# Expert weights of a mixture layer: split in the background by GpSimd, and blocks run by expert rank

## The reference

```python
# layer 1: attention of each token over itself and 77 context tokens (one head)
s_self = jnp.einsum('bsh,bsh->bs', q, k_tok)[..., None]
s_ext = jnp.einsum('bsh,beh->bse', q, k_ext)
probs = jax.nn.softmax(jnp.concatenate([s_self, s_ext], axis=-1), axis=-1)
ctx = probs[..., :1] * v_tok + jnp.einsum('bse,beh->bsh', probs[..., 1:], v_ext)
# layer 2: self-attention (16 heads of 32), and beside it 8 experts, 2 per token
attn = jax.nn.softmax(jnp.einsum('bqhd,bkhd->bhqk', q, k) / jnp.sqrt(hd), axis=-1)
attn_out = jnp.einsum('bhqk,bkhd->bqhd', attn, v).reshape(B, S, D)
gate = jax.nn.softmax(x @ W_gate + b_gate, axis=-1)
top_g, top_i = jax.lax.top_k(gate, TOP_K)
combine = jnp.sum(jax.nn.one_hot(top_i, E) * top_g[..., None], axis=2)
moe_out = jnp.einsum('bsef,bse->bsf', jnp.einsum('bsd,edf->bsef', x, W_experts) + b_experts, combine)
return attn_out + moe_out          # each expert's matrix is 512 x 512
```

## Time and profile before

| | us |
|---|---|
| median of 3 runs | 1459.54 |
| lowest, highest | 1453.82, 1528.65 |
| profiled execution, its own time | 1458.29 |
| its span, first to last instruction | 1456.7 |
| TensorE busy | 1324.4 (91%) |
| VectorE busy | 945.7 (65%) |
| ScalarE busy | 903.1 (62%) |
| GpSimd busy | 365.8 (25%) |

### The profile page before, as it was taken

One profiled execution on the slowest core, in us unless ns is written; L12 is line 12 of the kernel. 1 busy time (PEld: TensorE's weight loads), 2 busy tenths in 40 slices (PEclk: granted clock), 3 DMA queues, 4 the chain that ended last, 5 costly groups with the idle time before them and its releaser, 6 DMA issues.

```text
span 1456.7 us, 25076 instructions
## 1 busy us (share of the span) xinstructions
PE 1324.4 (91%) x6720; PEld 971.6 (67%) x6721; DVE 945.7 (65%) x2019; ACT 903.1 (62%) x1828; POOL 365.8 (25%) x580
## 2 busy tenths in 40 slices
PE   4989999999789899999999999999997769999997
PEld 4968888888565566565665656656563347777776
DVE  4256878787388877777777777777776734333432
ACT  4123434344258889899888998989997743333332
POOL 0001222221100040111101110011113027677775
PEclk9899999999899999999999999999997679999999
DMA  5004444447645344473454733447336277787774
GB/s 158 1 18 160 171 166 158 165 159 265 247 120 141 80 104 132 89 179 80 89 133 90 187 80 87 125 100 188 76 91 181 16 239 131 130 144 135 134 135 65
DMA packets 101293, 187.43 MB, mean 129 GB/s; under 512 B 27257, under 2 KB 35577, under 8 KB 99939
## 3 DMA queue, kind: packets, MB, share of 16 engines
q1 hardware_dynamic: 69984, 138.86, 33.1%
q0 software_dynamic: 26624, 42.04, 17.2%
q10 hardware_dynamic: 4611, 5.74, 1.4%
HBM read 71.09 MB, written 69.35 MB: 96 GB/s over the span
## 4 chain that ended last, share of the span: by engine, by line
PE 70%; issue 7%; ACT 7%; DMA 7%; DVE 6%; POOL 1%; ACTq 1%; POOLq 0%; SPq 0%; DVEq 0%
PE banks L216 14%; PE banks L218 13%; PE banks L217 13%; PE banks L1042 9%; PE banks L1026 6%; PE banks L1006 6%; ACT plain L732 3%; ACT banks L722 3%; DMA out_dram<-plain,score_bias 2%; DMA plain<-h_rows,score_bias 2%; PE banks L1099 2%; DVE plain L1465 1%; PE banks L894 1%; PE banks L927 1%; DMA plain<-in_L_xattn_Wq_dram 1%
## 5 line engine op out<-in xcount | busy, mean ns | idle before, releaser
L216 PE MATMUL banks<-parts 128*128 128x512 f32 (+6 forms) x1108 | 437.5, 395 | 30.0 <-issue 7.5
L218 PE MATMUL banks<-parts 128*128 128x512 f32 (+6 forms) x1108 | 423.8, 383 | 0.0
L217 PE MATMUL banks<-parts 128*128 128x512 f32 (+6 forms) x1108 | 423.8, 382 | 0.0
L1465 DVE TENSOR_REDUCE plain<-banks 128x1 f32<-128x512 f32 x512 | 329.1, 684 | 74.6 <-PE banks L1006 71.6
L722 ACT ACTIVATE banks<-banks,plain 128x512 f32<-128x512 f32 x512 | 338.7, 662 | 43.0 <-DVE plain L1465 40.6
L732 ACT ACTIVATE plain<-banks 128x1024 f32<-128x1024 f32 x256 | 262.5, 1026 | 40.9 <-PE banks L1026 39.2
L216 PEld LDWEIGHTS banks<-parts 128*128 128x128 f32 (+1 forms) x1108 | 214.4, 193 | 74.8 <-issue 36.5
L218 PEld LDWEIGHTS banks<-parts 128*128 128x128 f32 (+1 forms) x1108 | 214.0, 193 | 40.4
L217 PEld LDWEIGHTS banks<-parts 128*128 128x128 f32 (+1 forms) x1108 | 215.1, 194 | 34.4
L1006 PE MATMUL banks<-parts 96*128 96x512 f32 x512 | 208.9, 446 | 27.3 <-ACT banks L722 26.6
L1026 PE MATMUL banks<-parts 104*128 104x512 f32 x512 | 176.2, 426 | 15.1 <-ACT plain L732 14.0
(11 more groups left out here) (167 smaller groups left out, 1417.6 us busy)
## 6 DMA issues: line engine op xcount, KB each, us to landing
parts<-parts SPq DMA_DIRECT2D x384, 128.0 KB, 2.4
h_turned<-parts SPq DMA_DIRECT2D x32, 512.0 KB, 3.0
parts<-h_turned SPq DMA_DIRECT2D x32, 512.0 KB, 7.2
plain<-in_x_dram SPq DMA_DIRECT2D x32, 256.0 KB, 3.0
out_dram<-plain SPq DMA_DIRECT2D x32, 256.0 KB, 2.0
h_rows<-plain SPq DMA_DIRECT2D x32, 256.0 KB, 2.0
parts<-plain SPq DMA_DIRECT2D x8, 1024.0 KB, 4.6
out_dram<-plain POOLq DMA_DIRECT2D x16, 512.0 KB, 6.2
```

Source lines behind the costliest of these rows:

```text
L216: pe.matmul(out, stat[0], mov[0], start=first, stop=False)
L217: pe.matmul(out, stat[0], mov[1], start=False, stop=False)
L218: return pe.matmul(out, stat[1], mov[0], start=False, stop=last)
L1465: dve.tensor_reduce(nmx[:, k, t:t + 1], bank[SB[t]][:], AX.X, ALU.max, negate=True).then_inc(q["f_max"], 1)
```

## The change

- A new array in memory, `experts_split` (`ws_dram`), holds each expert's two parts. GpSimd fills it during the attention, expert by expert, in chunks of 128 rows: it loads a chunk (256 KB), rounds it, subtracts, and writes 512 KB (`load_chunk`, `split_chunk`). Experts 0 and 1 are split in batch 0, one in each of batches 1 to 5 (two chunks in each half), and the last in batch 6. The scatters of the list (`place`) run earlier: all 16 groups by batch 5.
- VectorE's routing ranks the experts by their number of blocks. Each rank has a fixed place in `parts`; blocks are run rank by rank.
- SP reads the list and loads the experts by rank in the last batch, each by one transfer of 2 MB whose address comes from a register. Rank 0 goes before the batch's stacks, the others as their places come free.
- The splitting of experts by ACT and DVE is gone, and so are ACT's four issues at step 6. ACT issues the biases' load after its last copy of the attention.
- PE's wait in the expert stage is for a count that is a constant per group of 8 blocks (`m_ready`). The loops of PE, ACT and DVE there hold 8 blocks in place of 4.
- GpSimd fetches the first four blocks' rows early in the last batch, before its last two `attended`.
- In `score` the key products come before the self-score products, with a semaphore of their own (`s_keys`).

```diff
-        EB = (0, EW, 3 * EW, r4 - EW, 2 * EW, r0, r4, r4 + EW)
+        EB = (0, r4 - EW, EW, 3 * EW, 2 * EW, r0, r4, r4 + EW)
+        chunk = [area(parts, r4 + EW + 4 * S + 2 * D * i, 2, D) for i in range(2)]
@@ sync @@
+            def load_expert(r):
+                if r == 0:
+                    sp.wait_ge(q["r_ranked"], 1)
+                    for i in range(2):
+                        sp.wait_ge(q[f"ws_out{i}"], 16 * NE * C // 2)
+                e = sp.value_load(ranked[0:1, r:r + 1], min_val=0, max_val=NE - 1)
+                sp.dma_start(ew[r], ws_dram[bass.ds(e, 1)].rearrange("e p n -> p (e n)")).then_inc(q[f"in_ew{r}"], 16)
...
                 sp.dma_start(V, Vst).then_inc(q["f_v_in"], 16)
+                if last:
+                    read_list()
+                    load_expert(0)
                 stacks(b, 1, 0, (0, 3), number(b, "R1")[0] + 1)
...
+                if last:
+                    load_expert(1)
+                    sp.wait_ge(q["f_d_full"], number(b, "R3")[0] + 1)
+                    load_expert(2)
+                    load_expert(3)
+                    for slot in (0, 1, 2, 4):
+                        sp.wait_ge(q[f"f_stack{slot}"], (2 * B if slot < 3 else B) * FILL)
+                    load_expert(4)
+                    sp.wait_ge(q["f_t_full"], T * (NH * b + 12))
+                    load_expert(5)
+                    sp.wait_ge(q["f_t_full"], T * (NH * b + 14))
+                    load_expert(6)
+                    sp.wait_ge(q["f_t_full"], T * (NH * b + NH))
+                    load_expert(7)
@@ gpsimd @@
+            def split_chunk(e, c):
+                n = e * C + c
+                pool.wait_ge(q[f"ws_in{c % 2}"], e * (C // 2 * 16) + c // 2 * 16 + 16)
+                pool.tensor_copy(chunk[c % 2][:, 0], full(chunk[c % 2][:, 1])).then_inc(q["ws_hi"], 1)
+                pool.wait_ge(q["ws_hi"], n + 1)
+                pool.tensor_tensor(chunk[c % 2][:, 1], full(chunk[c % 2][:, 1]), full(chunk[c % 2][:, 0]), ALU.subtract).then_inc(q["ws_lo"], 1)
+                pool.wait_ge(q["ws_lo"], n + 1)
+                pool.dma_start(ws_dram[bass.ds(e, 1)].rearrange("e p (a c n) -> p (e a) c n", a=2, c=C)[:, :, c, :],
+                               full(chunk[c % 2])).then_inc(q[f"ws_out{c % 2}"], 16)
...
+            with pool.Fori(1, B - 2) as b:
+                place(PER * b - PER + 1)
+                split_expert(b + 1, True, range(C // 2))
                 attended(b, 0)
+                for m in range(1, PER):
+                    place(PER * b - PER + 1 + m)
+                split_expert(b + 1, True, range(C // 2, C))
                 attended(b, 1)
...
             for i in range(4):
                 fetch(i)
+            attended(B - 1, 0)
             attended(B - 1, 1)
@@ scalar @@
-                    if last and k == 6:
-                        act.wait_ge(q["ew_moved"], 16)
-                        act.wait_ge(q["f_d_full"], number(b, "R3")[0] + 1)
-                        for e in range(EARLY):
-                            act.dma_start(full(ew[e][:, 1]), we_dram[e].rearrange("(c p) n -> p c n", p=P)).then_inc(q[f"in_ew{e}"], 16)
...
+            act.dma_start(be_all, b_exp.rearrange("(a e) n -> a (e n)", a=1).broadcast_to([P, NE * D])).then_inc(q["in_be"], 16)
@@ vector @@
-                            if last and k >= NH - 2 * EARLY:
-                                expert_lo((k - NH + 2 * EARLY) // 2, range(k % 2 * C // 2, (k % 2 + 1) * C // 2))
...
-            LATER = {0: over_tiles_1, 1: over_tiles_2, 2: over_tiles_3, 3: first_blocks_1, 4: first_blocks_2, 6: places, 7: first_records,
-                     8: second_records, 11: block_experts, 12: block_firsts, 13: block_order, 14: list_zero}
+            LATER = {0: over_tiles_1, 1: over_tiles_2, 2: over_tiles_3, 3: first_blocks_1, 4: first_blocks_2, 5: rank_places, 6: places, 7: first_records,
+                     8: second_records, 10: block_experts, 11: block_places, 12: block_firsts, 13: block_order, 14: list_zero}
@@ tensor @@
-                    if part == "first":
-                        e = pe.value_load(bexp[0:1, bass.ds(i, 1)], min_val=0, max_val=NE - 1)
-                        pe.wait_ge(q["m_elo"], e * C + C if k < 2 else NE * C)
+                    if k == 0:
+                        pe.wait_ge(q["m_ready"], n + 1)
```

More of the change, by code:

```diff
@@ L320, in program @@
         N_PICKED = 19
-        EARLY = NE // 2
+        U = 8
+        BULK = NB // U
+        assert NB % U == 0 and T * B * 2 >= U * NE
         @block.sync
@@ L420, in _ @@
             batch(B - 1, False, True)
[L422 to L435, removed]
+            for r in range(NE):
+                sp.wait_ge(q[f"in_ew{r}"], 16)
+                sp.sem_inc(q["m_ready"], BULK if r == NE - 1 else 1)
             for i in range(NB):
@@ L790, in blocks @@
             def blocks(n, part):
-                for k in range(4):
-                    i = 4 * n + k
-                    if not (part == "first" and k == 0) and not (part == "last" and k == 3):
+                for k in range(U):
+                    i = U * n + k
+                    if not (part == "first" and k == 0) and not (part == "last" and k == U - 1):
                         rows_hi(i + 1, (k + 1) % 2)
@@ L799, in _ @@
                 rows_hi(i, i)
-            for e in range(EARLY, NE):
-                expert_hi(e, range(C))
             blocks(0, "first")
-            with act.Fori(1, NB // 4 - 1) as n:
+            with act.Fori(1, BULK - 1) as n:
                 blocks(n, "middle")
-            blocks(NB // 4 - 1, "last")
-            weighted(NB - 1, 3, NB // 4 - 1)
+            blocks(BULK - 1, "last")
+            weighted(NB - 1, 3, BULK - 1)
         @block.tensor
@@ L897, in score @@
                                      start=False, stop=c == C - 1)
+                last.then_inc(q["s_keys"], 1)
+                for c in range(C):
+                    last = prod3(pe, bank[1][:, c * P:D], at(hT[u % 2], sl, c), at(A, sl, c, slice(c * P, D)), c == 0, c == C - 1)
                 last.then_inc(q["s_full"], 1)
@@ L1102, in blocks @@
             def blocks(n, part):
[L1103 to L1105 removed]
+                for k in range(U):
+                    i = U * n + k
+                    if part != "last" or k < U - 1:
                         await_ge(pe, "m_hT", i)
[L1108 removed]
+                        rows_turn(i + 1, U // 4 * n + (k + 1) // 4, k + 1)
                     pe.wait_ge(q["m_hT"], i + 1)
@@ L1122, in _ @@
             blocks(0, "first")
-            with pe.Fori(1, NB // 4 - 1) as n:
+            with pe.Fori(1, BULK - 1) as n:
                 blocks(n, "middle")
-            blocks(NB // 4 - 1, "last")
+            blocks(BULK - 1, "last")
         @block.vector
@@ L1370, in _ @@
             small = [row[:, 7 * NT + NE * i:7 * NT + NE * (i + 1)] for i in range(4)]
-            run, blk, start, base = (t_in, t_lg)[(NT - 1).bit_length() % 2], small[0], small[1 + NE.bit_length() % 2], small[3]
-            ends = small[2 - NE.bit_length() % 2]
+            run = (t_in, t_lg)[(NT - 1).bit_length() % 2]
+            blk, start, ends, base = small
+            ranks = t_sel.rearrange("p t e -> p (t e)")
+            pairs, key, rank, place_of = ranks[:, 0:NE * NE].rearrange("p (a b) -> p a b", a=NE), *(ranks[:, NE * (NE + i):NE * (NE + i + 1)] for i in range(3))
             def running(now, other, n, d=1, end=None):
```

131 lines of the change are left out of this document (74 added, 57 removed).

## The result

| | before | after |
|---|---|---|
| median (5 runs each) | 1455.30 us | 1468.78 us |
| lowest, highest | 1452.54, 1528.65 us | 1463.94, 1470.68 us |
| ratio after to before | | 1.0089, 95% interval 1.0058 to 1.012 |

The change made the kernel 0.9% slower. The forecast was 1445 us and the range ended at 1463; the direction was wrong. The profiled execution took 1468.78 us. The ratio leaves out one run of the kernel before (1528.65 us), which fell in a slower state of the chip.

A forecast was written before the change was run, and what follows sets the result against it. PE was taken to bound everything up to the last batch, and something else the last batch. Terms 0 + 4 + 1 - 11 - 7 + 0 = -13 took 1458.3 to 1445 us; range 1433 to 1463.

The forecast's parts named there:

- Splitting in the background: Attention: GpSimd's 32 chunks fit its time and nothing waits for them except `tmp`'s reuse; +1 us, from 0 to +5.
- PE bounds everything up to the last batch: Layer 1 and attention before the last batch: PE sets the pace; GpSimd's background work costs or saves only through others.
- Ranking: Batch 0: VectorE's added routing operations reach PE, near their plain sum of 3.8 us; +4 us, bounds +1.6 and +8.
- The row on shared memory access: Batch 0: GpSimd's passes delay VectorE's two-input SBUF operations, at most 4.4 us; by the skill's rule some 8 us.
- A chunk: GpSimd during attention: fetching, rounding, subtracting and writing one chunk takes about 10 us, at most 14.
- Key products first: Attention scores: VectorE may begin two small operations earlier per tile, PE does not wait for them; 0 us, -1 to +1.
- The last batch: Last attention batch: eight subtractions leave VectorE and ACT loses its issues; -11 us, from -14 to -5.
- the rival of PE's clock: Last batch: PE's low clock, not VectorE, sets the step, so only 5 us are won there: 1451 us; 12%.
- Start of the experts: Behind the attention: first fetch and add come earlier, ACT's and VectorE's splits go; -7 us, from -9 to 0.
- the stage itself: Expert stage: 72 blocks at 3.25 us, paced by GpSimd's unchanged queue; 0 us, from -3 to +2.
- The slower one: Attention: GpSimd does not keep up, chunks take 20 us and the attention loses 55 us: 1500 us; 5%.
- if batches grow: Attention: a sign of being wrong; batches 1 to 6 were to stay at 92.0 us between PV3 products.

The follow-up runs named there:

- experiment 9: Changed kernel with ScalarE's six middle attention batches written out in place of its loop, other engines' loops kept: 1447.96 us, ratio to the kernel before 0.9952.
- Quiet chunks: Changed kernel with the same chunks moved to times when SP copies nothing, first expert's load behind the last batch's stacks: 1446.85 us, ratio to the kernel before 0.9962.
- experiments 1 to 11: Variants of the changed kernel (splitting cut or moved, finer stack wait, loops written out), one of the kernel before with ScalarE's loop written out: 1436.63 to 1471.21 us.

## Why the prediction was wrong

- **Splitting in the background, +1 (0 to +5): this step failed.** It cost 23 to 28 us: the changed kernel lies 27.6 above the one without splitting by the medians, 23 by the ratios. I priced GpSimd's time, found that it fits, and asked who waits for GpSimd. Nobody does, and that was right: no chunk was ever late. I didn't ask who else fetches over the 16 engines in that time. "Over a DMA share of 0.50" was named and passed over as an average. Two things were short and on the path. The first is ScalarE's jump: 14.1 us, and 1.7 more in batch 3's last interval, all gone with the loop in experiment 9. Of these 9.3 are longer stops, and the rest goes with PE at 1.2 GHz behind them. The jump stood in the chain of the kernel before at all five places, beside a loop's line. So "PE bounds everything up to the last batch" was too strong as well: writing the loop out won 8.8 us with PE's work unchanged. The second is SP's stacks: in batch 1 the chain runs through SP's issues of the copies and one landing of 4.11 us (567.17), at batch 0's beginning through one of 5.87 us (418.34), where the chain of the kernel before has none at either place. Quiet chunks remove the batch 1 part: 22.08 and 23.21 us against 24.47 and 25.44. With ScalarE written out and the chunks left, 23.79 and 25.71 stay, so this part is not the jump's. Behind the late landing PE's clock is 0.50 for 6.8 us in both (from 571.6 and 569.2). That it is the stacks is read from the chain, no run took the copies away. The remaining 7 us or so are batch 0's late start (2.6), its step 9 to 13 (2.2 beyond the ranking's 0.6) and steps 5 to 9 of batches 2 to 5 (1.9).

- **Ranking, +4 (1.6 to 8): too high.** Batch 0's step 9 to 13 grew by 0.6 us without GpSimd's passes, by 2.8 us with them.

- **The row on shared memory access, and the Trainium skill's rule beside it: the better guide.** The rule, on "SBUF — State Buffer", section "Who interferes with whom", was weighed at up to 8 us, which was low by its own terms: a rounding and a subtraction measured 1.9 us, so 15 us for eight chunks. The arithmetic alone cost 8.9 us by the medians. In its profile batch 0 lost 2.5 us in one interval and started late by 5.9; of that start one run each is known, and it varies.

- **A chunk, 10 us, at most 14: right.** From one chunk's write to the next, where they follow each other at once, it is 7 to 13 us. A cast takes 0.63, the subtraction 1.28 (I had 0.5, and up to 2.0), the issues 0.57 and 0.72, the landings 4.9 and 4.4 us in the median.

- **Key products first, 0: right.** Layer 1's rows are the same.

- **The last batch, -11: right**, -10.5. The groups are 21.6 to 22.2 us, as forecast, and ScalarE's waits for maxima fell from 11.8 to 0.5 us. That PE's clock has no part in them is not so, though. In seven of the eleven other profiles of changed kernels one or two of these groups have a granted clock of 0.64 and take 23.7 to 24.0 us, where groups with 0.73 to 0.86 take 21.1 to 22.8. The last batch then takes 67.6 to 68.7 us in place of 65.8, a gain of 8 us and not 10.5. So the rival of PE's clock holds in part, and that the term was met to 0.5 us is partly luck.

- **Start of the experts, -7, and the stage itself, 0: right.** -6.7 together; the last `attended` took 8.17 us, one more than forecast, and PE waits once 1.9 us where it was 5.48. From the first add to the end it is 260 us. What lies behind the last group's start varies from 278 to 284 us over the profiles of experiments 1 to 11 (282.0 in the kernel before with ScalarE's batches written out), so one profile settles this term to a few us only.

- **The rivals.** None was what happened, apart from the part of PE's clock in the last batch. The slower one needed GpSimd to fall behind. I had "if batches grow" among the signs of being wrong, without a mechanism for it or a chance. The range was made from the terms' bounds, and the failed one had +5 for its upper end: about a fifth of its real size, 23 to 28.

## What to carry to other kernels

Work on an idle engine is free only if what it puts on the DMA engines is, and if its passes hold no other engine: ask which short transfers, and which instruction fetches, are on the path at that moment, and price their landing under load, not the idle engine's time. In the chain, an "issue" piece of over 1 us that repeats once per batch beside a loop's line can be a jump, and writing the loop out tells: here it won 8.8 us for one edited line of the kernel before. Its stop grows with traffic, and a stop long enough to leave PE idle costs PE's clock on top. Background transfers belong where nothing small is due; the same 24 MB cost 23 to 28 us in one place and 6 in another.

## What was not expected of the hardware

- A jump of ScalarE's loop stops it for 1.4 to 1.5 us, and with GpSimd's transfers in flight it stands still for 2.8 to 5.2 us. Writing out TensorE's, VectorE's and SP's loops as well won only 0.2 us more per batch (90.4 to 90.2).
- Behind most of the long stops PE's granted clock is 0.50 for 3.4 to 10.2 us (17 of 20 stops in four profiles); behind the stops of 1.5 us and less it stays at 1.00.
- A third of the bytes (fetches alone, 1471.2 us) disturbed as much as all of them (1471.2 without arithmetic).
- SP's copies of 128 KB land in 2.4 us, beside chunks in 4.6.
- VectorE's cast of four elements takes 0.17 us, and 1.2 when GpSimd is in a subtraction.
- With the expert blocks written out their stage was 10 us longer in the profiled run, the slowest of its six; whether that is the edit's doing is not shown.
